# Two more state rows on VectorE, their scans written over the decays in PSUM, with a first front spread over three PSUM banks and orders per stage

## The reference

```python
# M: a Mamba layer, E = 512 channels, 16 states
hidden, gate = split(n @ W_in)
hidden = silu(causal_conv4(hidden) + conv_bias)
dt, B, C = split(hidden @ W_x, [128, 144])
dts = softplus(dt @ W_dt + b_dt)
for t: state = exp(dts * A) * state + dts * B * hidden    # state: [E, 16]
       y[t] = sum over the 16 states of state * C
M = ((y + hidden * D) * silu(gate)) @ W_out
# F: 32 experts of width 96, the 8 best per token, softmax weights
F = sum over experts of w_e * (silu(n @ Wg_e) * (n @ Wu_e)) @ Wd_e
```

## Time and profile before

| what | us |
|---|---|
| median of 3 runs (lowest, highest) | 1367.48 (1365.01, 1369.09) |
| profiled execution | 1367.53 |
| its span in the trace | 1365.7 |
| closing add (L793) of the 1st block, of the last | 159.1, 1362.2 |
| softplus (L608) of the 1st block, of the last | 48.1, 1265.0 |

### The profile page before, as it was taken

One profiled execution on the slowest core, in us unless ns is written; L12 is line 12 of the kernel. 1 busy time (PEld: TensorE's weight loads), 2 busy tenths in 40 slices (PEclk: granted clock), 3 DMA queues, 4 the chain that ended last, 5 costly groups with the idle time before them and its releaser, 6 DMA issues.

```text
span 1365.7 us, 26543 instructions
## 1 busy us (share of the span) xinstructions
PE 1312.0 (96%) x9314; PEld 1233.5 (90%) x9314; DVE 1242.2 (91%) x1644; ACT 1193.1 (87%) x1990; POOL 1243.7 (91%) x625
## 2 busy tenths in 40 slices
PE   2599999999999999999999999999999999999998
PEld 2589999999999999999999999999999999999987
DVE  4598989999899999999999899999989999998987
ACT  3889899889889988999899989989998999988984
POOL 2789999999989999999999999999999999999996
PEclk9899999999999999999999999999999999999999
DMA  6544344534434544444444434434443444434442
GB/s 167 153 133 122 118 130 126 129 115 128 128 113 127 140 121 122 127 119 122 124 125 129 123 114 123 144 115 129 121 124 115 130 131 127 121 119 118 124 133 70
DMA packets 184533, 170.76 MB, mean 125 GB/s; under 512 B 42672, under 2 KB 167632, under 8 KB 184400
## 3 DMA queue, kind: packets, MB, share of 16 engines
q1 hardware_dynamic: 150608, 121.86, 30.7%
q10 hardware_dynamic: 33792, 47.20, 12.1%
HBM read 163.72 MB, written 5.24 MB: 124 GB/s over the span
## 4 chain that ended last, share of the span: by engine, by line
PE 53%; DVE 16%; POOL 12%; ACT 9%; issue 9%; ACTq 1%; SPq 0%; DMA 0%; DVEq 0%; POOLq 0%
PE pair_ps L849 22%; PE out_ps L967 12%; PE front_ps L849 7%; POOL state L468 6%; DVE state L750 5%; PE turn_ps L929 5%; PE out_ps L977 3%; ACT decay L546 3%; DVE acc L757 3%; POOL state L477 3%; POOL moe L483 2%; DVE u L767 2%; ACT L546 2%; DVE dt L738 2%; DVE moe L774 1%
## 5 line engine op out<-in xcount | busy, mean ns | idle before, releaser
L750 DVE TENSOR_TENSOR_SCAN state<-decay,state 128x512 f32<-128x512 f32 x512 | 615.0, 1213 | 70.6 <-ACT decay L546 67.4
L468 POOL TENSOR_TENSOR state<-du,b_rep 128x1024 f32<-128x1024 f32 x256 | 639.2, 2505 | 29.0 <-DVE u L767 28.9
L546 ACT ACTIVATE decay<-dt,neg_a 128x255 f32<-128x255 f32 x1024 | 437.2, 467 | 39.6 <-DVE state L750 27.2
L967 PE MATMUL out_ps<-w_down,moe 128*128 128x256 f32 x1536 | 353.0, 379 | 0.1
L483 POOL TENSOR_TENSOR moe<-moe,rw_rep 128x512 f32<-128x512 f32 x192 | 285.9, 1492 | 45.8 <-DVE moe L774 36.5
L967 PEld LDWEIGHTS out_ps<-w_down,moe 128*128 128x128 f32 x1536 | 283.1, 190 | 34.6 <-issue 0.5
L849 PE MATMUL pair_ps<-xnT_hi,w_up_hi 128*128 128x256 f32 x768 | 228.7, 298 | 8.9 <-ACT moe L554 8.7
L477 POOL TENSOR_TENSOR state<-state,c_rep 128x1024 f32<-128x1024 f32 x96 | 228.6, 2382 | 2.7 <-DVE state L750 2.7
L546 ACT ACT_TABLE_LOAD x176 | 225.8, 1283 | 3.1
L849 PE MATMUL pair_ps<-xnT_hi,w_gate_hi 128*128 128x256 f32 x768 | 223.2, 291 | 0.6 <-DVE moe L774 0.5
L849 PE MATMUL pair_ps<-xnT_hi,w_up_lo 128*128 128x256 f32 x768 | 217.6, 283 | 0.0
(11 more groups left out here) (112 smaller groups left out, 2055.2 us busy)
## 6 DMA issues: line engine op xcount, KB each, us to landing
w_down<-in_L_ffn_w_down_dram SPq DMA_DIRECT2D x384, 128.0 KB, 2.6
b_rep<-b_dram ACTq DMA_DIRECT2D x128, 256.0 KB, 3.4
rw_rep<-rw_dram SPq DMA_DIRECT2D x256, 96.0 KB, 2.6
rw_rep<-rw_dram SPq DMA_DIRECT2D x256, 64.0 KB, 2.7
c_rep<-b_dram ACTq DMA_DIRECT2D x96, 128.0 KB, 3.1
rw_rep<-rw_dram SPq DMA_DIRECT2D x256, 32.0 KB, 2.5
x_in<-L_attn_input_states_dram SPq DMA_DIRECT2D x16, 256.0 KB, 3.5
res<-L_attn_input_states_dram SPq DMA_DIRECT2D x16, 256.0 KB, 4.1
```

The costliest lines, as they stand in the source:

```text
L468: pool.tensor_tensor(state[:, n % STATES, :, :], du2[:, q, :, :], b_rep[:, n // BCH % 2, n % BCH, :][:, None, :].broadcast_to([P, ET, T]), ...
L546: last = act.activation(decay[:, h, j, 1:T], dt[:, q, e, 1:T], ACT.Exp, scale=neg_a[:, e, n:n + 1])
L750: dve.tensor_tensor_scan(x, decay[:, h, :, :].rearrange("p e t -> p (e t)"), x, 0.0, ALU.mult, ALU.add).then_inc(scanned, 1)
L967: last = pe.matmul(out_ps[:, c, :], moe[:, p % RING, j, c * P:(c + 1) * P], w_down[:, p % RING, j, :], start=(p == 0 and j == 0 and c == 0 ...
```

## The change

In words, with the names of the diff:

- BY_ROW gets states 5 and 9, so eight states are rows and eight are turned. For these two (ROWS_BY_VECTOR) the scan's output goes over its decays in PSUM, `row_product` multiplies it there by c_rep and `add_half` adds it into u2, all on VectorE and by halves. ScalarE's next decays for that half wait for the add, and zero one column again first (the one at the seam of the two channel groups). GpSimd's next input into the state buffer waits for the scan alone. The order of the row sums is fixed by ROW_SUMS. c_rep is loaded eight times per block at slots of its own (C_LOAD_AT).
- Normalising x_in goes from VectorE to ScalarE, as scale and bias (`shifted` on VectorE computes the bias, `normed` on ScalarE applies it). The router's last product goes to ScalarE too (`share`).
- The router (logits, weights) gets semaphores of its own. In block 0 hid1, lowT and dt1 use the first half of turn_ps, the router the second (`front_bank`), and its weights leave from acc.
- w_in is split by columns: the hidden half first (piece 0), the gate half as piece 13 (GATE_SPLIT). hid0 of block 0 waits for piece 0 alone.
- All slot lists come in three versions, for the first block, the middle blocks and the last (`stage`). PAIRS_BY_VECTOR is empty: no weighing moves.

```diff
-    BY_ROW = [n for n in range(NS) if n in ((2, 4, 6, 8, 10, 12))]
+    BY_ROW = [n for n in range(NS) if n in ((2, 4, 5, 6, 8, 9, 10, 12))]
...
-    FRONT = ["xnT", "hid0", "hid1", "logits", "weightsT", "low", "lowT", "dt0", "dt1"]
+    FRONT = ["xnT", "hid0", "hid1", "low", "lowT", "dt0", "dt1"]
+    ROUTER = ["logits", "weightsT"]
...
-    TURN_AT = [[12, 12], [17, 17], [28, 29], [49, 52], [67, 70], [79, 82], [107, 108], [116, 117], [120, 122], [127, 128]]
+    TURN_AT = [[[7, 11], [26, 31], [31, 42], [69, 73], [104, 104], [111, 113], [115, 119], [129, 129]],
+               [[13, 13], [21, 21], [41, 44], [69, 75], [94, 96], [110, 114], [123, 124], [124, 129]],
+               [[13, 13], [18, 20], [39, 39], [56, 56], [126, 126], [158, 165], [167, 170], [172, 175]]]
...
-    ROW_ADD_AT = [34, 44, 62, 77, 99, 121]
+    ROW_ADD_AT = [[36, 52, [40, 46], 61, 80, [74, 79], 102, 117], [39, 46, [42, 45], 62, 79, [74, 76], 101, 124], [34, 50, [43, 48], 67, 80, [75, 77], 104, 134]]
...
+    C_LOAD_AT = [[-22, 29, 30, 38, 47, 62, 81, 91], [-17, -5, 29, 43, 45, 63, 70, 92], [-12, 3, 32, 46, 49, 62, 81, 100]]
+    ROWS_BY_VECTOR = [n for n in BY_ROW if n in ((5, 9))]
+    ROW_SUMS = sorted(BY_ROW, key=lambda n: n if n in ROWS_BY_VECTOR else n + ROW_LAG)
...
-    SPLIT_SCALAR_AT = [-116, -115, -102, -91, -86, -84, -79, -77, -61, -60, -49, -38, -31, -25, -17, -5, 1, 12]
+    SPLIT_SCALAR_AT = [-125, -76, -75, -70, -65, -57, -53, -50, -49, -42, -16, -10, -7, -2, 2, 4, 4, 11]
...
+        def front_bank(i, name):
+            if i == 0 and name in ("hid1", "lowT", "dt1"):
+                return turn_ps[:, 0, :].rearrange("p (j t) -> p j t", j=2)
+            if i == 0 and name in ROUTER:
+                return turn_ps[:, 1, :].rearrange("p (j t) -> p j t", j=2)
+            return front_ps
...
                 if not (isinstance(i, int) and i == 0 and n < STATES):
-                    if before in BY_ROW:
+                    if before in ROWS_BY_VECTOR:
+                        pool.wait_ge(scanned, half_at(at, before, 1))
+                    elif before in BY_ROW:
                         pool.wait_ge(row_added, row_at(at, before))
...
             def decays(i, q, n, h):
-                if not (isinstance(i, int) and i == 0 and n == 0):
-                    act.wait_ge(scanned, half_at(i, n - 1, h))
+                before, of = (n - 1) % NS, i if n > 0 else i - 1
+                if before in ROWS_BY_VECTOR and of >= 0:
+                    act.wait_ge(row_summed, row_half(of, before, h))
+                    act.activation(decay[:, h, 1, 0:1], dt[:, q, 2 * h, 0:1], ACT.Copy, scale=0.0)
+                elif of >= 0:
+                    act.wait_ge(scanned, half_at(of, before, h))
...
+            def share(i):
+                act.wait_ge(rw_step, 3 * i + 3)
...
+                for c in range(TT):
+                    last = act.activation(rw[:, c, :], rest[:, c, :], ACT.Copy, scale=inv[:, c:c + 1])
+            def normed(i):
+                act.wait_ge(shift_ready, i + 1)
+                for c in range(TT):
+                    last = act.activation(x_in[:, c, :], x_in[:, c, :], ACT.Identity, bias=shift[:, c:c + 1], scale=rstd[:, c:c + 1])
...
-                dve.tensor_tensor_scan(x, decay[:, h, :, :].rearrange("p e t -> p (e t)"), x, 0.0,
-                                       ALU.mult, ALU.add).then_inc(scanned, 1)
+                a = decay[:, h, :, :].rearrange("p e t -> p (e t)")
+                dve.tensor_tensor_scan(a if n in ROWS_BY_VECTOR else x, a, x, 0.0, ALU.mult, ALU.add).then_inc(scanned, 1)
...
+            def row_product(i, n, h):
+                r = i * NR + BY_ROW.index(n)
+                dve.wait_ge(scanned, half_at(i, n, h))
+                dve.wait_ge(c_loaded[r % ROWS], (r // ROWS + 1) * 16)
+                x = decay[:, h, :, :]
+                dve.tensor_tensor(x, x, c_rep[:, r % ROWS, :][:, None, :].broadcast_to([P, 2, T]), ALU.mult).then_inc(row_ready[1], 1)
+            def add_half(i, q, n, h):
+                wait_summed(dve, i, ROW_SUMS.index(n) - 1, h)
+                row_multiplied(dve, i, n, h)
+                x = u2[:, q, 2 * h:2 * h + 2, :]
+                dve.tensor_tensor(x, x, decay[:, h, :, :], ALU.add).then_inc(row_summed, 1)
```

More of the change, by code:

```diff
@@ L73, in build @@
     UNITS = [(2 * g + k % 2, k // 2) for g in range(PAIRS // 2) for k in range(4)]
-    UNIT_AT = [0, 1, 5, 19, 21, 24, 37, 39, 45, 53, 55, 57, 59, 65, 65, 83, 83, 84, 106, 109, 109, 115, 122, 122]
-    OUT_AT = [38, 38, 48, 59, 72, 92, 95, 102, 118, 123, 143, 143]
-    TURN_AT = [[12, 12], [17, 17], [28, 29], [49, 52], [67, 70], [79, 82], [107, 108], [116, 117], [120, 122], [127, 128]]
-    TURN_Y_AT, PROJECT_AT = [130, 131], 155
-    PE_FRONT = {'xnT': -112, 'hid0': -106, 'hid1': -99, 'logits': -90, 'weightsT': -59, 'low': -56, 'lowT': -46, 'dt0': -44, 'dt1': -24}
@@ new lines, in build @@
+    TURN_Y_AT, PROJECT_AT = [[131, 137], [138, 138], [201, 207]], [157, 157, 235]
+    PE_FRONT = [{'xnT': -110, 'hid0': -96, 'hid1': -92, 'logits': -89, 'weightsT': -8, 'low': -44, 'lowT': -21, 'dt0': -13, 'dt1': -8},
+                {'xnT': -108, 'hid0': -105, 'hid1': -92, 'logits': -82, 'weightsT': -53, 'low': -46, 'lowT': -45, 'dt0': -42, 'dt1': -34},
+                {'xnT': -113, 'hid0': -107, 'hid1': -92, 'logits': -86, 'weightsT': -52, 'low': -48, 'lowT': -45, 'dt0': -39, 'dt1': -29}]
```

357 lines of the change are left out of this document (229 added, 128 removed).

## The result

The changed kernel takes 1378.34 us (median of 4 runs, 1377.25 to 1378.64), beside 1368.28 us for the kernel before on the same chip: a ratio of 1.0078, interval 1.0064 to 1.0092. It is slower by 10 us; the forecast was 1342, faster by 26. The profiled execution has a span of 1376.8 us.

What follows compares the result with a forecast made beforehand. TensorE was taken to bound the middle, busy 81.08 of 81.47 us per block. From 1367.5 us, 15.8 (middle), 8 (front) and 2 (end) were subtracted: 1341.7, so 1342 us, range 1330 to 1360.

Steps and rivals of the forecast that it cites:

- TensorE, 1.58 us per block: Middle blocks: states 5 and 9 lose 16 transposes, taking 1.58 us per block off TensorE; floor of the period 79.85 us.
- 77.3 forecast: VectorE's busy time per middle block: 76.74 + 5.39 for products and adds - 2.93 - 1.87 = 77.3 us.
- 75.9 forecast: ScalarE's busy time per middle block: 73.48 plus 2.4 us for normalising, router weights and zeroing; 22 table changes unchanged.
- 76.48 forecast: GpSimd's busy time per middle block, unchanged at 76.48 us: six products, sixteen inputs, twelve weighings.
- The period, 80.3 forecast: Middle blocks: from 81.43 to 80.3 us, near the 79.85 floor; 1.13 us for each of 14 periods, 15.8 us.
- the small shift comes: VectorE, middle blocks: the added shift and the router's removed product are both about 0.23 us and cancel.
- The two loads of c_rep: ScalarE's queue, two more loads per block: costed at nothing, covered by 4 us of ScalarE's idle time.
- Rival 1: Middle blocks: VectorE becomes the bound through late decays after states 5 and 9; middle gains nothing, 1357.5 us; chance 0.18.
- rival 2: Middle blocks: decays of states 6 and 10 expose product and add; period 82.8 us, total time 1377 us; chance 0.07.
- The front: First block: low at about 25 us, softplus 36, first scan 47.6 instead of 54.69; 8 us gained.
- rival 3: First block: lead lost to full engines and late splits; 1350 us; sign, closing add under 4 us before 159; chance 0.13.
- The end: Last block: an order of its own and 1.6 us of turns fewer; 2 us gained, ends 0 and 4.

Runs made afterwards that it cites:

- e6: The changed kernel with the shift behind both row-sum adds and, in middle blocks, ScalarE's normalising six slots later; 1367.98 us, ratio 1.0008 to the kernel before.
- e19: The changed kernel with c_rep's load for state 10 at slot 74 instead of 70; 1372.02 us, ratio 1.0035 to the kernel before.
- the reliefs: e6 with work cut on VectorE, GpSimd, ScalarE or TensorE alone (1361.85, 1369.61, 1366.06, 1364.82 us), or on all four together (1352.46 us).
- e4: Six rows and the kernel before's orders in middle and last blocks, with only the change's new first block; 1389.07 us, ratio 1.0161 to the kernel before.
- e3: The change's two vector rows in the kernel before's middle and last orders, normalising and router's last product on VectorE; 1542.94 us, ratio 1.1283 to the kernel before.

## Why the prediction was wrong, step by step

**TensorE, 1.58 us per block: right.** Busy time 81.08 to 79.35, and turns at the same rate. **VectorE: right, the sum partly by luck.** 77.3 forecast, 77.55 measured, products 0.695, adds 0.683 and scans in PSUM 1.224 us, all within the bounds given. But the six row sums, taken as unchanged, cost 1.304 us each in the middle instead of 1.556, 1.5 us less, and the shift 1.0 us more than its price: two misses that nearly cancel. **ScalarE:** 75.9 forecast, 75.19 measured. **GpSimd:** 76.48 forecast as unchanged, 73.14 measured, since inputs take 2.396 us instead of 2.503 and weighings 1.305 instead of 1.492, while its row products take 2.556 instead of 2.382. The count of 22 table loads per block is right. The amounts of work were not what failed.

**The period, 80.3 forecast, 82.51 measured.** The step that failed first is the sentence "The router's last product leaves and the small shift comes; both are of the size of L575's 0.23 us and cancel". The shift measured 1.19 us, and 0.67 of wait ahead of it, and above all it was costed as an amount without its place: between two adds that TensorE waits for, at the head of a wait of ScalarE's. The prediction asks of each added wait who stands behind it, and did not ask it of this one. Price, together with the place of ScalarE's normalising behind it: 0.9 us in every quiet block (e6). The rule that it cites from the Trainium skill (SBUF — State Buffer, "SBUF: two separate sides"), that of a VectorE instruction with two SBUF inputs and a GpSimd instruction that reads SBUF the one that starts first shuts out the other to its end, was applied to the new products, which it spares, and not to the new shift, whose two inputs are both in SBUF. The trace agrees: in all fifteen blocks in which the shift meets a GpSimd instruction it ends within 0.02 us of that one. In the first block:

```profile
52.84 2.36 DVE L814 SCALAR_TENSOR_TENSOR shift<-moments,rstd 128x2 f32<-128x2 f32 x1 [0.59 <-POOL rstd L535]
```

```profile
52.78 2.41 POOL L332 TENSOR_TENSOR w_in_lo<-dt,w_in_hi 128x1024 fp32r<-128x1024 f32 x1
```

The 128x2 operation ends at 55.20 us, GpSimd's at 55.19.

**The two loads of c_rep, "I cost this at nothing, covered by 4 us of ScalarE's idle time": wrong.** That idle time lies elsewhere. The load at slot 70 blocks ScalarE for 0.4 us with nothing to cover it, and for up to 2 us in some blocks: some 6.3 us of the run (e19), of them 3.7 in the long ones of the twelve periods. Of the 26.5 us by which these twelve missed the forecast (12 x 2.21), the place of the shift and the normalising explains 12 x 0.9 = 10.8 and the long blocks 3.7; the other 12, 1.0 per block, are quiet periods of 81.3 against 80.3. (The whole miss, 1378.6 for the profiled execution less 1341.7, is 36.9: 26.5 here, 2.8 in the second block, 3.5 of the lead, 3.5 in the last two blocks and 0.6 behind.)

**"Between the floor 79.85 and the old 81.43 I take 80.3 ... since the old order got within 0.4 us of its own": wrong.** The old order came that close because the others had slack beside it. With four engines at 90 to 98% the new one doesn't: even without the two mistakes above TensorE idles for 2 us per block, and the reliefs say that this is not one engine's load. The prediction saw the risk ("every in-order wait that TensorE's slack hid ... is now closer to it") and charged 0.45 us for it. Measured are 82.51 - 79.85 = 2.66 us per block: 0.9 for the place of the shift and the normalising, 0.3 for the long blocks, and 1.5 (81.3 against 79.85) whose cause stays open. This term of the sum is the one that was mis-sized. Rival 1 named the outcome that the middle gains nothing and gave it 0.18, with a mechanism, late decays after states 5 and 9, that didn't occur; rival 2's time of 1377 is near the result by another road.

**The front: right up to the first scan, half lost behind it.** Lines of the first block, from the chain and from VectorE's timeline:

```profile
24.28 4.43 PE front_ps L1029 x16
...
34.52 1.28 ACT L722
```

```profile
46.21 1.22 DVE L868 TENSOR_TENSOR_SCAN state<-decay,state 128x512 f32<-128x512 f32 x1 [0.36 <-ACT decay L641]
```

low at 24.28 (25 forecast), softplus at 34.52 (36), the first scan at 46.21 (47.6), 8.5 us ahead of before. But the closing add is only 4.5 ahead. The windows of 40 to 80 us:

```profile
40.00:60.00 20.00, 10.97 (x60) 10.26 (x59) 15.69 (x17) 15.65 (x29) 19.92 (x11) 0.76 0.49 132
60.00:80.00 20.00, 15.12 (x80) 13.81 (x80) 16.98 (x27) 15.64 (x28) 17.57 (x9) 0.77 0.57 152
```

GpSimd is busy for 19.92 of 20 us: inputs, the splits that now fall here and block 1's statistics share it. TensorE is granted a clock of 0.77 from 60 to 80 us instead of 0.89 and gets through 80 matmul records instead of 105. That looks like rival 3's mechanism at half its size (its own sign, a closing add less than 4 us before 159, did not come); I read it from the trace, and no run takes it apart, since e4 failed to.

**The end, 2 us forecast:** the last two blocks took 145.3 us instead of 144.9. The last order brings 3.4 us in the 15th block (76.0 against 79.4) and gives 3.7 back in the 16th (69.2 against 65.5).

## What to carry to other kernels

Cost an added instruction by its place before its size: between two steps that another engine waits for, its own wait and duration go onto that engine's path, and 0.2 us of work can be 2 us of time. An instruction that issues a transfer occupies the engine that issues it: 0.3 to 0.4 us here, now and then up to 2; put it under a table load or a long instruction, not ahead of what an engine waits for. And when several engines stand near their limits, neither the busiest one's floor nor a list of its waits says what a saving brings; look at which engine holds the chain, and at single periods, since a mean over blocks hides rare long ones.

## What the runs showed of the hardware that was not expected

An issue on ScalarE's queue has a median of 0.33 us, and takes 0.9 to 2.4 us in one to nine of 288 per run in the kernels with the change's middle orders; SyncE's issue of the same moment is long too (2.27 instead of 0.90 us for two). Every slow one overlaps a 16 KB packet of the kind instruction on queue q8; in the kernel before, where such packets are as frequent (74 in the run against 72), none of its issues is slow. What else must come together the traces don't show. The Trainium skill (DMA: Bandwidth & Descriptors, "Issuing engines are not separate DMA queues") calls the time to initiate a transfer usually small relative to the transfer; against the 3.4 us from issue to landing of c_rep 0.33 is a tenth, but 2.00 is not, and it is the engine's time that counted here.

GpSimd's mean times moved with nothing changed in its instructions: inputs 2.505 to 2.396 us and weighings 1.492 to 1.305, but row products 2.382 to 2.556. The medians hardly moved (2.386 and 2.388, 1.292 and 1.282, 2.383 and 2.382), so it is a few stretched ones that became fewer or more. Whether the PSUM operands of VectorE's new rows or the new orders did it is not separated: e3, two rows in the old orders, lies between for inputs and weighings (2.439, 1.350), with row products at 2.407, and e4, six rows in them, is at 2.502, 1.497 and 2.410. And the same 128x2 operation took from 0.160 to 2.356 us within one run, by what was left of the GpSimd instruction that it met.
